# A graph network kernel: two pieces of seven gathers, four slots for edge indices, and node passes in four stages

## The chip, the cores and the metric

The kernel runs on one core of one Trainium2 chip. Its figure is the device time of the whole program in microseconds (us), lower is better. Three runs of the kernel before gave 2862.45 us as median (2857.86 to 2866.96).

## The reference

The graph has 6250 nodes with 128 features and 100000 edges, given as `src` and `dst`, sorted by `dst`, with 16 attributes each. Two layers follow one another, each with a residual and a layer norm around it:

```python
# layer 0: attention over the edges, then a two-layer perceptron per node
q, k, v = X @ Wq, X @ Wk, X @ Wv                      # 8 heads of 16
scores  = einsum(q[dst], k[src]) / sqrt(16)
alpha   = segment softmax of scores over dst
emb     = segment_sum(alpha * v[src], dst) @ W0
h1      = layer_norm(X + emb) * g1 + b1
x       = layernorm(X + layer_norm(h1 + relu(h1 @ fc1 + b) @ fc2 + b) * g2 + b2)
# layer 1: messages; the first 50000 edges use W1f/W2f, the others W1b/W2b
h       = relu(concat(x[src], edge_attr, req) @ W1 + b1) @ W2 + b2
h       = x * (1 + eps) + segment_sum(h, dst) of both halves
out     = layernorm(x + relu(h @ Wu + bu))
```

Both layers read a node's row once per edge (`[src]`) and add into rows by `dst`.

## The kernel before

The edges are cut into chunks of 1792, that is 14 tiles of 128 edges. After a setup (q, k, v of all nodes written to a table in memory, index tables built) three stages follow.

**First loop** (attention, 56 chunks). GpSimd (POOL) issues 14 indirect DMAs per chunk (L657), one per tile of 128 edges, each fetching k and v of 128 source nodes into one of four slots (`RING`). TensorE (PE) expands the queries of a chunk with one matmul per tile (`queries`, L1050), VectorE (DVE) multiplies them with the gathered keys (L1386) and sums by head (L1388), and after some scans by segment weights the values (L1440, two halves). PE then adds the 14 tiles of a chunk into one PSUM area (L1090, a product with a 0/1 mask) and raises `l_agg`; ScalarE (ACT) copies that area (L832). The work of a pass is spread over several chunks: a pass does the scores of `new`, the weights of `b_`, the averages of `c_`. The numbers of `PIECES` (L47) cut a chunk's 14 tiles into four pieces of 4, 3, 4 and 3 tiles. One piece is one pair L1386/L1388, one PSUM bank of queries and one semaphore of the gathers. `gather_chunk` (L643 on) waits ahead of its pieces: for the chunk's indices (`l_ix`) and the second half of the weighted values of the chunk whose slot it takes (`l_pvb`) at the start, for `l_agg` before the second piece, for the queries (`l_q`) before the third, for the turned chunk ends (`l_lr`) before the last.

**Node passes** (10 groups of 5 tiles of nodes). `passes3` runs passes over the groups in three stages on each engine: in one pass `new` gets its embedding matmul (L1132) and first norm, `mid` the perceptron (L1115, ACT relu L868, L1142), `old` the second and third norm, then transposes (L1110), their copy (ACT L903), the product with W1 (L1152), the copy of that (ACT L906) and the store to the table `y_tab` (SP L474). The next pass begins with the transposes of h1 (L1110) and their copy (ACT L881).

**Second loop** (messages, 57 preparations, 56 chunks). POOL gathers rows of `y_tab` (L710), again 14 per chunk into four slots. PE turns the attributes (`attr_T`) and multiplies them with W1 (`attr`, L1187), DVE adds gathered rows and that product (L1575), ACT applies relu (L940), PE adds into rows by `dst` (L1200) and raises `m_agg` behind the last. The indices, columns and attributes of a chunk have two slots. SP loads them: `next_attr` when the attributes of an earlier chunk have been turned, `load_edges(new + 2)` (SP L501, L502) when all four pieces of chunk `new` have been summed (`m_hid`) and its columns read (`m_dcr`). `gather_edges` (L700 on) waits for the indices `m_ix[u]` and for `m_agg` of the chunk that held the slot, before the second piece for `m_eTp` and before the third for `m_u`.

All semaphores, registers and the order on each engine are written out by hand; no planner decides anything.

## Time and profile before

| | |
|---|---|
| median of 3 runs | 2862.45 us |
| profiled execution | 2882.01 us, its span 2880.1 us |
| mean granted TensorE clock | 0.711 of full speed |
| PE matmul / weight load busy | 1588.5 us (55%) / 1255.8 us (44%) |
| DVE / ACT busy | 1430.9 us (50%) / 746.1 us (26%) |
| POOL busy | 1566.9 us (54%) |
| DMA | 255.22 MB, mean 89 GB/s |

The rows below are of the profiled execution. Times there are microseconds from its start. "idle before, releaser" tells how long an engine had been idle ahead of an instruction and what ended it; "issue" is time in which it waited for nothing that the profile shows, "remote" a semaphore whose raiser the profile could not name. An indirect DMA's time on POOL is the time in which it is issued, not that in which the data arrives. One matmul of the program on float32 appears as several instructions.

### The profile page before, as it was taken

The page shows a single profiled execution, that of the slowest core. Times are in us where ns is not written, and L with a number is a line of the kernel's source. Part 1 is how long each engine was busy: PE and PEld are TensorE (multiplying, and loading weights), DVE is VectorE, ACT ScalarE, POOL GpSimd, SP SyncE. Part 2 cuts the span into 40 slices and gives each one's busy share as a digit, 9 for nine tenths or more (in the row PEclk, how much of TensorE's full clock was granted, in tenths as well). Part 3 has the DMA queues.
Part 4 walks back from the last instruction along what each step waited for, and adds up shares of the span by engine and source line. Part 5 has one row for each costly group of instructions (what it writes and reads, how often), then busy time and mean ns, then how long its engine had stood idle before and what let it go on. Part 6 is the DMA issues. An engine that isn't in the chain of part 4 may idle for free.

```text
span 2880.1 us, 32266 instructions
## 1 busy us (share of the span) xinstructions
PE 1588.5 (55%) x7344; PEld 1255.8 (44%) x7345; DVE 1430.9 (50%) x2992; ACT 746.1 (26%) x1502; POOL 1566.9 (54%) x1648
## 2 busy tenths in 40 slices
PE   5315556565556565555777345555555555555546
PEld 3215555555555555554555233333433333333424
DVE  3226666666666666666555234343443333344435
ACT  2213333333333333333454111111111111111111
POOL 3346666666666666663111455655666665556653
PEclk8557676767776777776998667766676666666667
DMA  5474444444444444441000112211221121112211
GB/s 167 138 200 127 143 131 141 131 138 133 129 142 131 141 131 138 133 128 60 18 27 27 56 42 51 52 49 48 54 51 51 50 52 50 47 48 51 53 49 38
DMA packets 148162, 255.22 MB, mean 89 GB/s; under 512 B 73948, under 2 KB 99088, under 8 KB 147996
## 3 DMA queue, kind: packets, MB, share of 16 engines
q0 software_dynamic: 65072, 160.39, 19.9%
...
q8 instruction: 12, 0.20, 0.0%
...
## 4 chain that ended last, share of the span: by engine, by line
issue 33%; PE 22%; DVE 16%; another core or an unknown queue 13%; DVEq 5%; DMA 5%; ACT 4%; SPq 1%; POOL 0%; ACTq 0%; POOLq 0%
PE ps L1090 8%; PE ps L1050 6%; DVE arena L1566 3%; DVE arena L1435 2%; DVE arena L1575 2%; PE ps L1200 2%; DVEq L1595 2%; PE ps L1187 1%; ACT arena L873 1%; PE ps L1152 1%; DVEq L1594 1%; DVE arena L1440 1%; DMA first<-d 1%; DVEq L1592 1%
## 5 line engine op out<-in xcount | busy, mean ns | idle before, releaser
L710 POOL DMA_INDIRECT arena<-y_tab,arena x784 | 741.9, 946 | 512.6 <-issue 494.1
L657 POOL DMA_INDIRECT arena<-kvq_tab,arena x784 | 749.0, 955 | 471.3 <-issue 240.6
L1050 PE MATMUL ps<-arena 128*128 128x128 f32 x1596 | 325.7, 363 | 331.0 <-issue 251.4
L1200 PEld LDWEIGHTS ps<-arena 128*128 128x128 f32 x1568 | 285.5, 247 | 413.2 <-issue 394.1
L1200 PE MATMUL ps<-arena 128*128 128x128 f32 x1568 | 308.0, 336 | 282.8 <-issue 273.5
L1050 PEld LDWEIGHTS ps<-arena 128*128 128x128 f32 x1596 | 299.5, 275 | 349.9 <-issue 345.5
L1090 PE MATMUL ps<-arena 128*128 128x136 f32 x1568 | 319.2, 391 | 173.3 <-DVE arena L1440 88.5
L1090 PEld LDWEIGHTS ps<-arena 128*128 128x128 f32 x1568 | 309.5, 295 | 190.6 <-issue 190.6
L940 ACT ACTIVATE arena<-arena 128x512 f32<-128x512 f32 x224 | 118.9, 567 | 1029.7 <-DVE arena L1575 662.7
L1575 DVE TENSOR_TENSOR arena<-ps,arena 128x512 f32<-128x512 f32 x224 | 127.8, 616 | 511.2 <-remote 299.1
L1187 PE MATMUL ps<-w1blk,eaT 113*128 x456 | 271.3, 677 | 59.4 <-issue 55.6
L809 ACT ACTIVATE arena<-arena 128x1792 f32<-128x1792 f32 x58 | 191.5, 3301 | 0.0
L1568 DVE TENSOR_REDUCE arena<-arena 128x128 f32<-128x1792 f32 x57 | 182.4, 3200 | 2.0
L1404 DVE COPY arena<-arena 8x1 f32<-8x1 f32 x56 | 7.9, 141 | 337.5 <-ACT arena L843 337.5
L832 ACT ACTIVATE arena<-ps 128x136 f32<-128x136 f32 x56 | 16.0, 285 | 507.4 <-remote 476.9
L1388 DVE TENSOR_REDUCE arena<-arena 128x32 f32<-128x512 f32 x224 | 139.2, 621 | 8.4 <-issue 0.5
L1386 DVE TENSOR_TENSOR arena<-ps,arena 128x512 f32<-128x512 f32 x224 | 135.9, 607 | 5.7 <-remote 3.0
L1187 PEld LDWEIGHTS ps<-w1blk,eaT 113*128 113x128 f32 x456 | 90.9, 240 | 75.1 <-issue 74.9
L1566 DVE TENSOR_TENSOR arena<-ps,arena 128x1792 f32<-128x1792 f32 x57 | 114.3, 2006 | 4.8 <-ACT arena L930 4.8
L1440 DVE TENSOR_TENSOR arena<-arena,ps 128x896 f32<-128x896 f32 x112 | 115.6, 1068 | 0.0
L1435 DVE TENSOR_TENSOR arena<-ps,arena 128x1792 f32<-128x1792 f32 x56 | 112.3, 2005 | 0.0
L1601 DVE TENSOR_TENSOR arena<-arena,ps 128x128 f32 x56 | 16.2, 288 | 190.2 <-issue 179.7
...
## 6 DMA issues: line engine op xcount, KB each, us to landing
...
```

The lines of the kernel that those rows point to most:

```text
L657: g.indirect_dma_start(kv_s[:, r, t, :], None, kvq_tab.rearrange("n (a d) -> (n a) d", a=3), bass.IndirectOffsetOnAxis(ap=v3(idx, RING)[:, ...
L710: g.indirect_dma_start(yg_s[:, r, t, :], None, y_tab, bass.IndirectOffsetOnAxis(ap=v3(idx1, 2)[:, u, t:t + 1], axis=0)).then_inc(m_g[r][k] ...
L809: a.activation(hotT.rearrange("n (u g e) -> n u g e", u=2, g=G)[:, u, :, :], line.rearrange("n (e g) -> n g e", g=G), ACT.Relu, scale=-1.0 ...
L1050: last = mm(bank(k)[:, t * D:(t + 1) * D], hotT_s[:, u, s0 + t, :], v3(qwin, 2)[:, u, :])
L1090: last = mm(sums, hot_s[:, u, t, :], contrib_s[:, u, t * RW:(t + 1) * RW], start=(t == 0), stop=(t == G - 1))
L1187: mm(bank(j)[:, 0:n * D], eaT_s[:, u, k * P:(k + 1) * P], w1blk[:, ds(way + a0 * D, n * D)]).then_inc(m_u, 1)
L1200: last = mm(bank(6 + u)[:, 0:W], yg_s[:, r, t, :], hot1_s[:, u, t, :], start=(t == 0), stop=(t == G - 1))
L1435: tt(hot_s[:, u, :, :], columns[:, None, :].to_broadcast([P, G, P]), dcr_s[:, u, :, None].to_broadcast([P, G, P]), ALU.is_equal).then_inc( ...
L1440: tt(contrib_s[:, u, s0:s1, :, 0:DH], kv_s[:, r, s0:s1, D:2 * D].rearrange("p g (h w) -> p g h w", h=H), weights.rearrange("p (g h) -> p g ...
L1566: link(tt(hot1_s[:, u, :, :], columns1[:, None, :].to_broadcast([P, G, W]), dcr1[:, :, None].to_broadcast([P, G, W]), ALU.is_equal))
L1568: v.tensor_reduce(v3(hsum, 2)[:, u, :], hot1_s[:, u, :, :].rearrange("p g n -> p n g"), AX_X, ALU.add).then_inc(m_hot, 1)
L1575: tt(rows_, v3(bank(j)[:, 0:n * D], n), rows_, ALU.add).then_inc(m_hid, 1)
```

## The change

There are three parts.

1. `PIECES` is now two pieces of seven tiles in both loops. A piece's queries or attribute products lie in a pair of PSUM banks, and the DVE and ACT instructions of a piece cover 896 elements per partition in place of 512 or 384. In the first loop PE does the queries of seven tiles ahead of the sums L1090 and seven behind (as before), and DVE's order within a pass changes: `averages`, `steps` and `lanes` now stand ahead of the wait for ACT's exponentials (`l_e`), and one of the two score pieces comes last. `gather_chunk` is not edited, but with two pieces it never comes to its waits ahead of a third and fourth: it waits for `l_ix` and `l_pvb` at the start and for `l_agg` ahead of the eighth tile (the fifth before), and not for `l_q` and `l_lr`.
2. In the second loop the indices, columns and attributes have four slots. SP loads all three of chunk `new + 4` after the hidden rows of chunk `new`, and the first four before the node passes. The gathers of a chunk wait only at its start.
3. The node passes have four stages: the product with W1 of a group (`out_`), its copy and its store are in the pass after that of its last norm. The order within a pass changes on PE, ACT and DVE. POOL's two memsets for the second loop come after its first addition.

The diff, cut to its core. `...` marks what is left out (declarations, the same edits of indices elsewhere, the shape of L1386 and L1575):

```diff
-PIECES = ((0, 4), (4, 3), (7, 4), (11, 3))
+PIECES = ((0, 7), (7, 7))
...
-            with eng.Fori(0, GROUPS - 2) as i:
-                one_pass(i + 2, i + 1, i)
-            one_pass(None, GROUPS - 1, GROUPS - 2)
-            one_pass(None, None, GROUPS - 1)
+            one_pass(0, None, None, None)
+            one_pass(1, 0, None, None)
+            one_pass(2, 1, 0, None)
+            with eng.Fori(0, GROUPS - 3) as i:
+                one_pass(i + 3, i + 2, i + 1, i)
+            one_pass(None, GROUPS - 1, GROUPS - 2, GROUPS - 3)
+            one_pass(None, None, GROUPS - 1, GROUPS - 2)
+            one_pass(None, None, None, GROUPS - 1)
...
+            sp.wait_ge(l_over, 4)
+            sp.wait_ge(s_eac, 32)
+            sp.wait_ge(s_tabi[1], 48)
+            def load_chunk(chunk, r):
+                off = sp.value_load(tab_sb[1][0:1, ds(5 * chunk, 1)], min_val=0, max_val=NB * CH)
+                sp.dma_start(eat_s[:, r, :], ea1[ds(off, CH), :].rearrange("(p g) f -> p (g f)", g=G)).then_inc(m_at[r], 16)
+                sp.dma_start(v3(idx1, RING)[:, r, :], i1[ds(off, CH)].rearrange("(p g) -> p g", g=G)).then_inc(m_ix[r], 16)
+                sp.dma_start(v3(dcol1, RING)[:, r, :], d1[ds(off, CH)].rearrange("(p g) -> p g", g=G)).then_inc(m_ld[r], 16)
+
+            for c in range(RING):
+                load_chunk(c, c)
...
             def sp_msgs(r, new, a_, b_, c_):
                 u = r % 2
                 if new is not None:
-                    next_attr(new + 3, 1 - u)
                     sp.wait_ge(s_eac, 32)
                     sp.wait_ge(m_hid, spent)
-                    sp.wait_ge(m_dcr, prepared)
-                    load_edges(new + 2, u)
+                    load_chunk(new + RING, r)
                     sp.reg_add(spent, spent, NP_)
-                    sp.reg_add(prepared, prepared, 1)
+                    if r == RING - 1:
+                        sp.reg_add(loaded, loaded, 16)
...
             def gather_edges(r):
-                u = r % 2
                 pool.wait_ge(m_buf, 4)
-                pool.wait_ge(m_ix[u], landed)
+                pool.wait_ge(m_ix[r], landed)
                 pool.wait_ge(m_agg, slot_free)
                 for k, (s0, n) in enumerate(PIECES):
-                    if k in (1, 2):
-                        pool.wait_ge(m_buf, 4)
-                        pool.wait_ge(*((m_eTp, turned_) if k == 1 else (m_u, asked)))
                     for t in range(s0, s0 + n):
                         g.indirect_dma_start(yg_s[:, r, t, :], None, y_tab,
-                                             bass.IndirectOffsetOnAxis(ap=v3(idx1, 2)[:, u, t:t + 1], axis=0)).then_inc(m_g[r][k], 16)
+                                             bass.IndirectOffsetOnAxis(ap=v3(idx1, RING)[:, r, t:t + 1], axis=0)).then_inc(m_g[r][k], 16)
                 pool.reg_add(slot_free, slot_free, 1)
-                pool.reg_add(asked, asked, NP_)
...
-            def act_pass(new, mid, old):
+            def act_pass(new, mid, old, out_):
                 if new is not None:
                     a.activation(v3(nTa, GRP), by_tile(new), ACT.Copy).then_inc(n_aT, 1)
                 if mid is not None:
                     act.wait_ge(n_hTp, mid + 1)
                     a.activation(nTh, bank(0, 2)[:, 0:GRP * P], ACT.Copy).then_inc(n_hT, 1)
-                    relu(mid, 0)
                 if old is not None:
                     sqrt(1, old, norm2)
+                if out_ is not None:
+                    act.wait_ge(n_y, out_ + 1)
+                    act.wait_ge(n_yfree, out_ + 1)
+                    y_ = yst[:, ds((out_ % 2) * (GRP * 2 * D), GRP * 2 * D)]
+                    a.activation(y_[:, 0:(GRP - 1) * 2 * D], bank(2, 2)[:, 0:(GRP - 1) * 2 * D], ACT.Copy)
+                    a.activation(y_[:, (GRP - 1) * 2 * D:GRP * 2 * D], bank(1)[:, D:3 * D], ACT.Copy).then_inc(n_ys, 1)
                 if mid is not None:
-                    relu(mid, 1)
-                if mid is not None:
-                    relu(mid, 2)
-                    relu(mid, 3)
+                    for c in range(FC):
+                        relu(mid, c)
                 if old is not None:
                     sqrt(2, old, norm2)
-                if new is not None:
-                    sqrt(0, new, norm1)
-                if old is not None:
                     act.wait_ge(n_r[1], old + 1)
                     normalised(v3(res2, GRP), v3(res2, GRP), norm2).then_inc(n_x1, 1)
                 if new is not None:
+                    sqrt(0, new, norm1)
                     act.wait_ge(n_r[0], new + 1)
                     normalised(v3(res, GRP), v3(res, GRP), norm1).then_inc(n_n1, 1)
                 if old is not None:
                     act.wait_ge(n_xTp, old + 2)
                     act.wait_ge(n_x1c, old + 1)
                     a.activation(nTx, bank(0, 2)[:, 0:GRP * P], ACT.Copy).then_inc(n_xT, 1)
-                    act.wait_ge(n_y, old + 1)
-                    act.wait_ge(n_yfree, old + 1)
-                    a.activation(yst[:, ds((old % 2) * (GRP * 2 * D), GRP * 2 * D)], bank(4, 3)[:, 0:GRP * 2 * D], ACT.Copy).then_inc(n_ys, 1)
...
                 if new is not None:
                     queries(w, 0, True)
-                    queries(w, 1, True)
...
                 if new is not None:
-                    queries(w, 2, True)
-                    queries(w, 3, True)
+                    queries(w, 1, True)
...
-            def pe_pass(new, mid, old):
+            def rows_y(t):
+                return bank(2, 2)[:, t * 2 * D:(t + 1) * 2 * D] if t < GRP - 1 else bank(1)[:, D:3 * D]
+
+            def pe_pass(new, mid, old, out_):
                 if mid is not None:
                     pe.wait_ge(n_h1, mid + 1)
+                    if out_ is not None:
+                        pe.wait_ge(n_xT, out_ + 1)
                     transposes(h1, n_hTp)
+                if old is not None:
+                    pe.wait_ge(n_z, old + 1)
+                if out_ is not None:
+                    pe.wait_ge(n_xT, out_ + 1)
+                    for t in range(GRP):
+                        if t == GRP - 1 and mid is not None:
+                            pe.wait_ge(n_hT, mid + 1)
+                        last = mm(rows_y(t), nTx[:, t * P:(t + 1) * P], w1x[:, :])
+                    last.then_inc(n_y, 1)
+                if mid is not None:
                     pe.wait_ge(n_hT, mid + 1)
-                    pe.wait_ge(n_ys, 1 if old is None else old + 1)
                     hidden(mid, 0)
                     hidden(mid, 1)
-                if mid is not None:
-                    pe.wait_ge(n_f1s, mid * FC + 1)
-                    hidden(mid, 2)
+                if out_ is not None:
+                    pe.wait_ge(n_ys, out_ + 2)
                 if new is not None:
                     pe.wait_ge(n_aT, new + 1)
                     for t in range(GRP):
                         last = mm(bank(0, 2)[0:NT, t * D:(t + 1) * D], nTa[:, t * NT:(t + 1) * NT], w0_sb[:, :])
                     last.then_inc(n_emb, 1)
                 if mid is not None:
-                    pe.wait_ge(n_f1s, mid * FC + 2)
-                    hidden(mid, 3)
-                    pe.wait_ge(n_f1s, mid * FC + FC)
-                    if old is not None:
-                        pe.wait_ge(n_v[1], old + 1)
+                    for c in range(2, FC):
+                        pe.wait_ge(n_f1s, mid * FC + (c - 1))
+                        hidden(mid, c)
                     for t in range(GRP):
+                        if t == GRP - 2 and old is not None:
+                            turn_rows(new, old)
                         for c in range(FC):
+                            if t == 0:
+                                pe.wait_ge(n_f1s, mid * FC + (c + 1))
                             last = mm(bank(2, 2)[:, t * D:(t + 1) * D], v3(ffT, FC)[:, c, t * P:(t + 1) * P], fc2_sb[:, c, :],
                                       start=(c == 0), stop=(c == FC - 1))
                     last.then_inc(n_f2, 1)
-                if old is not None:
-                    if new is not None:
-                        pe.wait_ge(n_v[0], new + 1)
-                    pe.wait_ge(n_x1, old + 1)
-                    transposes(res2, n_xTp)
-                    pe.wait_ge(n_xT, old + 1)
-                    for t in range(GRP):
-                        last = mm(bank(4, 3)[:, t * 2 * D:(t + 1) * 2 * D], nTx[:, t * P:(t + 1) * P], w1x[:, :])
-                    last.then_inc(n_y, 1)
...
```

The change moves instructions in the three places that follow. A row is a line, an operation, the tiles that it writes and reads, and the semaphores it waits for; "x3" means three such in a row.

POOL in the second loop, one chunk's 14 gathers, before and now (`m_ix1` is the semaphore of the index slot, `m_buf` one raised once before the loop):

```order
L710 DMA arena<-y_tab,arena 128x128 [waits m_agg,m_ix1,m_buf]
L710 DMA arena<-y_tab,arena 128x128 x3
L710 DMA arena<-y_tab,arena 128x128 [waits m_eTp,m_buf]
L710 DMA arena<-y_tab,arena 128x128 x2
L710 DMA arena<-y_tab,arena 128x128 [waits m_u,m_buf]
L710 DMA arena<-y_tab,arena 128x128 x6
```
```order
L697 DMA arena<-y_tab,arena 128x128 [waits m_agg,m_ix1,m_buf]
L697 DMA arena<-y_tab,arena 128x128 x13
L699 REGISTER_ALU
L697 DMA arena<-y_tab,arena 128x128 [waits m_agg,m_ix2,m_buf]
L697 DMA arena<-y_tab,arena 128x128 x13
```

The two waits inside the chunk have gone, and each chunk's 14 gathers stand in a row behind one instruction that waits; now two chunks are shown, with other index slots.

DVE in a pass of the first loop, from the wait for `l_e` on before, and from the averages on now (L1412 and L1417 are the averages that were L1426 and L1431, L1353 the steps, L1390 the copy that waits for `l_e`, L1421 the mask, the L1426 of now the weighting that was L1440, L1372 and L1374 the scores that were L1386 and L1388; `...` stands for registers and the rest of the averages and steps):

```order
L1404 COPY arena<-arena 8x1 [waits l_paqc,l_lr,l_e]
...
L1405 SCALAR_TENSOR_TENSOR arena<-arena,ps 8x128 [waits s_dv]
...
L1426 SCALAR_TENSOR_TENSOR arena<-ps,arena 1x136 [waits l_avT,l_ra,l_cur]
...
L1431 TENSOR_TENSOR arena<-arena 128x128 [waits s_dv]
L1367 TENSOR_TENSOR arena<-arena 128x15 [waits l_ld3,s_init]
...
L1435 TENSOR_TENSOR arena<-ps,arena 128x1792 [waits l_dcr]
L1440 TENSOR_TENSOR arena<-arena,ps 128x56x16 x2
L1386 TENSOR_TENSOR arena<-ps,arena 128x4x128 [waits l_q,l_g2_2]
L1388 TENSOR_REDUCE arena<-arena 128x4x8 [waits l_prod]
```
```order
L1412 SCALAR_TENSOR_TENSOR arena<-ps,arena 1x136 [waits l_avT,l_ra,l_cur]
...
L1417 TENSOR_TENSOR arena<-arena 128x128 [waits s_dv]
L1353 TENSOR_TENSOR arena<-arena 128x15 [waits l_ld3,s_init]
...
L1390 COPY arena<-arena 8x1 [waits l_paqc,l_lr,l_e]
...
L1391 SCALAR_TENSOR_TENSOR arena<-arena,ps 8x128 [waits s_dv]
...
L1421 TENSOR_TENSOR arena<-ps,arena 128x1792 [waits l_dcr]
L1426 TENSOR_TENSOR arena<-arena,ps 128x56x16 x2
L1372 TENSOR_TENSOR arena<-ps,arena 128x7x128 [waits l_q,l_g2_1]
L1374 TENSOR_REDUCE arena<-arena 128x7x8 [waits l_prod]
```

The averages and steps now come ahead of the instruction that waits for `l_e`, and behind it the mask and the weighting follow directly on the across-chunk scans.

PE in a steady node pass: before, its end, and now, its beginning (L1142 is the second layer of the perceptron, L1110 and now L1082 are transposes, L1152 and now L1106 the product with W1, L1087 the first layer):

```order
L1142 MATMUL ps<-fc_sb,arena 128x128 [waits n_v1,n_f1s]
L1142 MATMUL ps<-fc_sb,arena 128x128 x19
L1110 MATMUL ps<-ident,arena 128x128 [waits n_x1,n_v0]
L1110 MATMUL ps<-ident,arena 128x128 x4
L1152 MATMUL ps<-w1x,arena 128x256 [waits n_xT]
L1152 MATMUL ps<-w1x,arena 128x256 x4
```
```order
L1082 MATMUL ps<-ident,arena 128x128 [waits n_xT]
L1082 MATMUL ps<-ident,arena 128x128 x4
L1100 REGISTER_ALU
L1106 MATMUL ps<-w1x,arena 128x256 [waits n_xT,n_z]
L1106 MATMUL ps<-w1x,arena 128x256 x3
L1106 MATMUL ps<-w1x,arena 128x256 [waits n_hT]
L1087 MATMUL ps<-arena,fc_sb 128x512 [waits n_hT]
```

The product with W1 has moved from the end of the pass to the place behind the first transposes of the next one, where it serves the group of the pass before. The transposes of the last norm's result (behind L1142 before) now stand inside the second layer's matmuls, ahead of their last eight.

## Rows read from the trace of the kernel before

**Rows 1.** The page: busy time of each engine.
```profile
PE 1588.5 (55%) x7344; PEld 1255.8 (44%) x7345; DVE 1430.9 (50%) x2992; ACT 746.1 (26%) x1502; POOL 1566.9 (54%) x1648
```

**Rows 2.** Busy time by stretch: PE, weight loads, DVE, ACT, POOL; clock, DMA share, GB/s.
```profile
600.00:800.00 200.00, 118.47 (x597) 108.25 (x598) 129.49 (x284) 72.54 (x128) 126.54 (x133) 0.71 0.45 137
1400.00:1600.00 200.00, 137.87 (x703) 103.32 (x703) 104.61 (x396) 95.04 (x172) 25.40 (x18) 0.87 0.08 29
2200.00:2400.00 200.00, 106.54 (x442) 74.67 (x441) 80.72 (x118) 27.64 (x81) 119.85 (x128) 0.67 0.20 50
```

**Rows 3.** Single lines: durations, first and last start, forms.
```profile
L1435 DVE TENSOR_TENSOR arena<-ps,arena x47: 2004/2005/2007, 314.2 to 1280.0; 128x1792 f32<-128x1792 f32 x47
L1566 DVE TENSOR_TENSOR arena<-ps,arena x49: 2004/2005/2006, 1721.8 to 2791.0; 128x1792 f32<-128x1792 f32 x49
L878 ACT ACTIVATE arena<-nodes x7: 1360/1361/1365, 1404.2 to 1543.6; 128x625 f32 x7
```

**Rows 4.** Waits from 300 to 1300 us: total, times, longest.
```profile
ACT arena L832 <- remote: 450.5, 48, 10.3
POOL arena L657 <- remote: 175.5, 48, 3.9
```

**Rows 5.** Timeline of a first-loop cycle: start, duration, instruction, idle before.
```profile
1233.05 0.95 POOL L657 DMA_INDIRECT arena<-kvq_tab,arena  x1 [3.63 <-remote]
...
1235.09 0.14 DVE L1404 COPY arena<-arena 8x1 f32<-8x1 f32 x1 [6.78 <-ACT arena L843]
...
1239.90 2.06 DVE L1440 TENSOR_TENSOR arena<-arena,ps 128x896 f32<-128x896 f32 x2
...
1241.11 5.15 PE L1090 MATMUL ps<-arena 128*128 128x136 f32 x28 [2.84 <-DVE arena L1440]
...
1249.35 0.95 POOL L657 DMA_INDIRECT arena<-kvq_tab,arena  x1 [0.31 <-issue]
1249.43 0.27 PE L1050 MATMUL ps<-arena 128*128 128x128 f32 x1 [1.82 <-issue]
...
1253.28 0.29 ACT L832 ACTIVATE arena<-ps 128x136 f32<-128x136 f32 x1 [9.30 <-remote]
...
1254.04 0.95 POOL L657 DMA_INDIRECT arena<-kvq_tab,arena  x1 [3.74 <-remote]
```

**Rows 6.** Timeline in the second loop, 2162 to 2255 us.
```profile
2162.52 0.37 PE L1200 MATMUL ps<-arena 128*128 128x128 f32 x1 [2.46 <-issue]
...
2186.52 0.34 SPq L501 DMA_DIRECT2D arena<-i  x1
...
2187.22 1.91 PE L1200 MATMUL ps<-arena 128*128 128x128 f32 x8
...
2188.97 0.95 POOL L710 DMA_INDIRECT arena<-y_tab,arena  x1 [8.74 <-issue]
...
2211.45 0.95 POOL L710 DMA_INDIRECT arena<-y_tab,arena  x1 [5.14 <-issue]
...
2254.81 0.95 POOL L710 DMA_INDIRECT arena<-y_tab,arena  x1 [8.65 <-issue]
```

**Rows 7.** Timeline of a steady node pass, 1469 to 1492.5 us.
```profile
1469.65 0.68 ACT L903 ACTIVATE arena<-ps 128x640 f32<-128x640 f32 x1
...
1470.38 2.43 PE L1152 MATMUL ps<-w1x,arena 128*128 128x256 f32 x10 [1.68 <-ACT arena L903]
1470.64 0.83 DVE L1538 TENSOR_TENSOR arena<-arena,rows 128x640 f32<-128x640 f32 x1
...
1472.65 0.71 PE L1110 MATMUL ps<-ident,arena 128*128 128x128 f32 x5
...
1475.38 0.70 ACT L881 ACTIVATE arena<-ps 128x640 f32<-128x640 f32 x1
...
1484.46 4.73 PE L1142 MATMUL ps<-fc_sb,arena 128*128 128x128 f32 x40 [0.89 <-ACT arena L868]
...
1487.87 3.96 ACT L873 ACTIVATE arena<-arena 128x128 f32<-128x128 f32 x10
...
1492.46 1.16 PEld L1152 LDWEIGHTS ps<-w1x,arena 128*128 128x128 f32 x6 [1.92 <-ACT arena L903]
```

**Rows 8.** Timeline where the second loop begins.
```profile
1600.63 0.28 SPq L474 DMA_DIRECT2D y_tab<-arena  x1
1607.44 0.20 ACT L913 ACTIVATE mark<-eps_ln 128x1 f32<-128x1 f32 x1 [7.14 <-DMA y_tab<-arena]
1609.35 0.29 DVE L1562 COPY ps<-iota_row 128x128 f32<-128x128 f32 x1 [10.14 <-issue]
...
1611.82 0.36 SPq L501 DMA_DIRECT2D arena<-i  x1
...
1614.21 0.99 POOL L710 DMA_INDIRECT arena<-y_tab,arena  x1 [18.46 <-DMA arena<-i]
...
1677.69 0.94 POOL L710 DMA_INDIRECT arena<-y_tab,arena  x1 [11.20 <-issue]
```

148 lines of the change are left out of this document (60 added, 88 removed).

## The prediction

> **What bounds the kernel now.** I read the busy times first: no engine is above 55% of the span [rows 1]. By stretch it is the same everywhere: in the first loop POOL is at 126.54 of 200 us and DVE at 129.49, in the second POOL at 119.85 and PE at 106.54, and in the node passes PE at 137.87 [rows 2]. So nothing is full, and what counts is who waits for whom.
>
> First loop. L1435 runs once per chunk: 47 of them from 314.2 to 1280.0 us, so a chunk takes 965.8 / 46 = 21.0 us [rows 3]. POOL waits 48 times, 175.5 us in all, for something "remote", so 3.66 us per chunk, and ACT's copy L832 waits as often and for up to 10.3 us [rows 4]. The timeline shows what that is. POOL resumes at 1233.05 and issues 14 gathers, the last at 1249.35 (14 x 0.95 us with 0.31 between, 17.3 us), then stands until 1254.04 [rows 5]. It waits for `l_agg`: L832, which waits for it too, starts at 1253.28. The matmuls L1090 that raise it are drawn from 1241.11 to 1246.26, 7 us earlier. In between PE's instructions come late, one at 1249.43 after an idle time of 1.82 us, and L832 starts only 3.0 us after the last gather has been issued at 1250.30 [rows 5]. The second loop shows the same more plainly: at 2162.52, inside a run of gathers, a matmul of 0.37 us comes after 2.46 us of nothing, while at 2187.22, with POOL at rest, eight take 1.91 us [rows 6]. So while POOL issues gathers for long, PE crawls, and what waits for PE's semaphores is set free when POOL stops. A chunk costs 14 gathers, 17.3 us, plus the pause that PE needs: 3.7 us in the first loop.
>
> Second loop. L1566 gives (2791.0 - 1721.8) / 48 = 22.3 us per chunk [rows 3]. The pauses are uneven. The starts behind them are 2188.97, 2211.45 and 2254.81: a run of 14 gathers takes 22.48 us with its pause of 5.14, one of 28 takes 43.36 with 8.65, that is 21.68 per 14 [rows 6]. The first run of the loop had 42 and took 1677.69 - 1614.21 = 63.48 us, 21.16 per 14 [rows 6, 8]. What ends the 8.74 us pause is the index load at 2186.52, issued once the hidden rows of the chunk two before were done: POOL starts 2.45 us behind it [rows 6].
>
> Node passes. Seven copies L878 from 1404.2 to 1543.6 give 139.4 / 6 = 23.2 us per pass [rows 3].
>
> **The change part by part.** The profiled execution took 2882.01 us, its span 2880.1; the median of three runs is 2862.45, that is 0.9932 of it. I sum in the profiled time and scale at the end.
>
> *First loop, pieces and waits: 0.* The gathers wait for `l_agg` once per chunk before and now, only ahead of another tile, so a cycle is still 14 gathers and a pause. The waits for `l_q` and `l_lr` that go released nothing late: none of POOL's long waits comes from them [rows 4]. The start of a chunk's gathers, now 7 gathers (8.8 us) after POOL resumes, needs `l_pvb`, the end of L1440. It ended 1241.96 - 1233.05 = 8.9 us after, but DVE now does about 2 us of averages and steps ahead of the wait for `l_e` in which it stood idle for 6.78 us [rows 5], so it ends at about 7. L1090 moves forward by the same 2 us, to end about 11 us after POOL resumes. If its semaphore still comes out only when POOL has stopped, nothing is won. Halving the number of DVE and ACT instructions per piece saves work beside idle time. Bounds: if `l_agg` comes out early, POOL runs on for two or three chunks at a time as in the second loop, at 21.16 to 22.48 per chunk against 21.0 [rows 3, 6, 8], so -0 to +1.4 us by some 52 chunks, at most +77; on the other side a pause shorter by the 2 us of DVE's work would give 52 x 2 = -104. I take 0, because the pause of 48 of 48 cycles is the same.
>
> *Second loop, slots: -39.* POOL no longer waits for an index load behind the hidden rows of the chunk two before. It waits for `m_agg` of the chunk four before, so it may run further ahead. In a pause such as that to 2188.97 the step from SP's load to the first gather (2.45 us) goes, and late in its place is the last L1200 of the older chunk, at about 2187.2 to 2189 [rows 6]. That takes 0 to 2 us from a pause per two chunks, and the share of long runs grows. 42 gathers took 21.16 per 14, 28 took 21.68, 14 took 22.48. I take 21.5 against 22.3 for all but the first and last chunks: 0.75 x 52 = -39. The bounds: 20.5 (17.3 with the 3.2 per chunk left if 2 us go from 5.14) gives 52 x -1.8 = -94; and if every pause were as long as 8.65 behind only 14 gathers (17.3 + 8.65 = 25.95), +190. The price is nearest to the run of 42.
>
> *SP's loads.* Each chunk now loads attributes, indices and columns together after its hidden rows, for a slot that is needed four chunks on. Three issues of 0.34 us stand on SP where POOL no longer listens closely. 0, hidden by the ring. The wait is behind nothing but the output store.
>
> *PE's attributes and the pair of banks.* As many columns and instructions as before. 0.
>
> *Node passes: -33.* The chain of a pass runs from ACT's copy L903 back to itself. Behind L903, which ends at 1470.33, PE does L1152, ACT copies it and the next nodes, and only then comes L881 at 1475.38 [rows 7]: 5.05 us. h1 is there at 1470.64 + 0.83 = 1471.47 and its transposes take 0.71, so L881 could start at 1472.2. With the product in the next pass, behind those transposes, 5.05 becomes about 1.9: -3.2. At the end of the pass ACT did ten L873 of 0.4 us (3.96 us from 1487.87) after all of DVE's statistics; now the five of `old` come first, beside DVE's work on `new`, and -1.4 to -2 is gained, part of which the scale operations between them give back. What is late next is the relus and the second layer, 4.73 us from 1484.46 [rows 7], with the product's 2.43 us now ahead of the first layer, which gives back up to 1 us. I take -4.6 per pass for seven passes, -32, and -1 for the filling, where POOL's first addition no longer stands behind two memsets. The extra pass at the end holds only work that was at the end before: 0. Bounds: -2 per pass (the first layer waits for the product) and -6, so -14 to -43.
>
> *Start of the second loop: -4.* The store of `y_tab` is known to be done at 1607.44, then SP loads attributes, then indices at 1611.82, and the first gather is at 1614.21 [rows 8]. The loads now lie ahead of the node passes, so the gather can follow DVE's L1562 at 1609.35, at about 1609.8: -4.4.
>
> Sum: 2882 + 0 - 39 - 33 - 4 = 2806, times 0.9932 = 2787; I forecast 2785 us.
>
> The Trainium skill ("SBUF — State Buffer", section "SBUF: two separate sides") says that engine ports and DMA ports are disjoint, and that neither a DMA nor a compute operation can slow the other. This trace does not bear it out for PE beside POOL's gathers: a matmul of 0.37 us comes after an idle 2.46 us in a run of gathers, and eight in 1.91 us outside one [rows 6]. By the rule a PE wait would not depend on POOL; the rival D below is what that gives.
>
> **The rivals.**
>
> A. The loops do not gain. The pauses are PE's drain, not the index load, and each is as long as before. For it: the pause grows with the length of the run (5.14 behind 14, 8.65 behind 28 [rows 6]), so running ahead costs what it brings. Against it: the 2.45 us between SP's load and POOL. Then only node passes and start count: 2862 - 37 = 2825.
>
> B. Slower: POOL is no longer held back, and PE crawls longer. Place: both loops. In the first the earlier L1090 gets its semaphore out before PE slows down, POOL runs on for 28 gathers, and a chunk costs 22.0 in place of 21.0: +1.0 x 52 = +52. In the second POOL is always a full ring ahead, so it is set free one chunk at a time and pays a pause behind each 14, the 5.14 of the row and some 0.5 because the last piece is now seven tiles (23.0 in place of 22.3): +0.7 x 52 = +36. Less 37: 2862 + 88 - 37 = 2913. It decides from about +0.7 us per chunk in both loops on. For it: runs of 14 are the dearest per gather in the second loop and L1090 now ends about 2 us earlier. Against it: none of the 48 pauses of the first loop was missed [rows 4].
>
> C. Running ahead pays more: 20.8 us per chunk in the second loop gives 52 x -1.5 = -78, and half a microsecond less pause in the first gives -26; with the node passes 2862 - 104 - 37 = 2721, taken as 2735.
>
> D. PE and DMA do not disturb each other, POOL's 14 gathers of 1.25 us are the only floor: 17.5 per chunk in both loops, 52 x (3.5 + 4.8) = -432, so about 2400. The crawl in rows 5 and 6 speaks against it.
>
> E. The four stages do not shorten a pass, because ACT's order is as tight as before, and the loops stay: 2858.
>
> **How the numbers follow.** Forecast 2785 (2755 to 2812): 0.40. A: 0.21. B: 0.20. C: 0.13. D: 0.02. E: 0.04. A measurement of this kernel can tell 0.3% (9 us) from no change. Faster by more is the forecast, A but for a small tail, C, D and a part of B that ends below 2854: 0.75. Slower by more is most of B: 0.19. Within it: E and the tails, 0.06. The range of 2710 to 2900 holds forecast, A, E, most of C and the lower half of B.
>
> **What would show it.** First loop: L1435's successor still every 21.0 us, with 14 gathers per run and a pause near 3.7; runs of 28 would show B. Second loop: no gather behind an index load, fewer runs of 14, under 21.8 us per chunk. Node passes: seven to eight passes at 18 to 19.5 us, with the relus or the second layer in the waits. First gather of the second loop 2 to 3 us after the store is known to be done. I am wrong if the interval in either loop moves by more than 1 us, since that weighs more than the node passes.

## The result and the profile after

The changed kernel takes 2906.88 us (median of four runs, 2884.57 to 2919.74), the kernel before 2860.84 (2857.86 to 2866.96): ratio 1.015, 95% interval 1.008 to 1.022. It is slower, where I had forecast 2785 us. The execution whose trace is read here took 2899.43 us with a span of 2897.2.

Three stretches tell where it went. The rows are POOL's gathers of the first loop, ACT's node copies and POOL's gathers of the second loop in the profile after (count, shortest, median and longest in ns, then first and last start). L649, L858 and L697 are what L657, L878 and L710 were.

```profile
L649 POOL DMA_INDIRECT arena<-kvq_tab,arena x784: 942/948/1157, 113.7 to 1431.3; - x196
L858 ACT ACTIVATE arena<-nodes x10: 1358/1362/1372, 1479.4 to 1626.3; 128x625 f32 x7, 128x625 f32<-128x625 f32 x3
L697 POOL DMA_INDIRECT arena<-y_tab,arena x784: 941/947/1072, 1687.6 to 2848.2; - x196
```

From the first gather to the first node copy it is 1365.6 us (1242.5 before, from 112.9 to 1355.4), from there to the second loop's first gather 208.2 (258.8), from there to the end 1209.6 (1265.9). So the first loop lost 123, the node passes won 51, the second loop 56: with 1 us at the start that is the 17 us between the two spans. The runs' medians differ by 46. The profiled execution of before was a long one: its 2882.01 us lie 15 above the longest of the four timed runs (2866.96), while the profiled one of the changed kernel is the second fastest of its four. So these stretches understate the loss and overstate one gain. Later runs tell how much: kernels below that keep the second loop of before took 1254.5, 1255.2 and 1251.6 us for it (e11, e14, e17), and those with four pieces and the old waits took 1225.8 to 1229.9 for the first loop (e12, e15, e16). Against these the first loop lost 136 to 140 us, the second won 42 to 46, and the node passes 52 to 53, which gives about 41 of the 46.

**First loop.** The waits between 300 and 1400 us (total, times, longest) show two new ones and one in place of the 175.5 us of [rows 4]:

```profile
ACT ps L821 <- remote: 290.8, 24, 15.5
...
POOL arena L649 <- DVE arena L1426: 174.3, 36, 9.2
...
POOL arena L649 <- remote: 46.9, 16, 3.4
```

The even pause of 3.7 us for `l_agg` [rows 4] has become uneven and rarer: ahead of a chunk's eighth tile POOL stops 23 times, for 2.4 to 6.2 us (the last row has 16 of them, the profile puts the others down to PE). At the start of a chunk it waits for DVE's weighting L1426 (`l_pvb`), 36 times and up to 9.2 us. The timeline of one such cycle (start, duration, instruction, idle before):

```profile
526.70 0.95 POOL L649 DMA_INDIRECT arena<-kvq_tab,arena  x1 [9.10 <-DVE arena L1426]
...
529.94 0.29 ACT L812 ACTIVATE arena<-ps 128x136 f32<-128x136 f32 x1 [2.87 <-PE ps L1063]
...
531.41 0.27 PE L1039 MATMUL ps<-ident,arena 128*8 128x128 f32 x1
...
546.49 0.36 ACT L821 ACTIVATE ps<-arena 128x112 f32<-128x112 f32 x1 [15.53 <-remote]
...
547.29 0.14 DVE L1390 COPY arena<-arena 8x1 f32<-8x1 f32 x1 [10.47 <-ACT arena L823]
...
548.17 1.99 DVE L1421 TENSOR_TENSOR arena<-ps,arena 128x1792 f32<-128x1792 f32 x1
...
550.09 2.06 DVE L1426 TENSOR_TENSOR arena<-arena,ps 128x896 f32<-128x896 f32 x2
...
552.97 0.95 POOL L649 DMA_INDIRECT arena<-kvq_tab,arena  x1 [9.03 <-DVE arena L1426]
```

Here the `l_agg` copy (L812) comes promptly, 3.2 us after POOL resumed. What is held is the next semaphore, `l_lr`: PE's transposes that raise it (L1039) are drawn at 531.41, and ACT's exponentials, which wait for it and for nothing else that is late, start at 546.49. POOL's last gather was over at 543.94 (552.97 - 9.03), 2.6 us earlier. Only then come exponentials, scans, mask and weighting, 6.5 us in all, and POOL, which has gathered its 14 tiles without a stop, needs just these weighted values to begin the next chunk. A cycle is 26.3 us: 17.2 of gathers and 9.05 of pause. Between such cycles lie stretches of the old kind, as this one:

```profile
674.11 0.95 POOL L649 DMA_INDIRECT arena<-kvq_tab,arena  x1 [2.56 <-remote]
...
681.73 0.95 POOL L649 DMA_INDIRECT arena<-kvq_tab,arena  x1 [0.30 <-DVE arena L1426]
...
694.77 0.95 POOL L649 DMA_INDIRECT arena<-kvq_tab,arena  x1 [2.88 <-remote]
```

They take 20.7 us, a little less than before; the weighted values come in just as the seventh gather begins (681.62 and 681.73), one before they are needed. But in the first loop's chunks 12 to 55, 30 of 44 times the weighted values came after POOL could have begun with them (slack: end of the gather before, plus the 0.3 us between two, less the end of L1426's second half), 15 times more than 5 us after. In the trace of before the slack was 3.2 to 4.7 us and never negative. The first 56 gathers also ran in one piece, followed by a pause of 56 us, where before there were 21, 28 and 7: the 57th comes 126.1 us after the first (105.8 before). What cut the first 56 before was the wait for the queries (`l_q`), ahead of a third piece. In the trace of before:

```profile
143.40 0.95 POOL L657 DMA_INDIRECT arena<-kvq_tab,arena  x1 [4.18 <-remote]
...
206.32 1.09 POOL L657 DMA_INDIRECT arena<-kvq_tab,arena  x1 [28.13 <-PE ps L1050]
```

**Node passes.** Two copies that open steady passes, 17.19 us apart (23.2 before [rows 3]):

```profile
1574.70 1.36 ACT L858 ACTIVATE arena<-nodes 128x625 f32 x1
...
1576.74 2.43 PE L1106 MATMUL ps<-w1x,arena 128*128 128x256 f32 x10
1576.87 0.71 ACT L861 ACTIVATE arena<-ps 128x640 f32<-128x640 f32 x1 [0.80 <-PE ps L1082]
...
1586.07 2.05 ACT L853 ACTIVATE arena<-arena 128x128 f32<-128x128 f32 x5 [0.45 <-DVE arena L1483]
...
1591.31 0.68 ACT L884 ACTIVATE arena<-ps 128x640 f32<-128x640 f32 x1
...
1591.89 1.36 ACT L858 ACTIVATE arena<-nodes 128x625 f32 x1
```

**Second loop.** The first gather follows the known end of the table's store by 2.0 us (6.8 before [rows 8]), and the pauses have shrunk from 5.1 and 8.7 us [rows 6] to these:

```profile
1678.80 0.28 SPq L489 DMA_DIRECT2D y_tab<-arena  x1
1685.62 0.20 ACT L891 ACTIVATE mark<-eps_ln 128x1 f32<-128x1 f32 x1 [7.15 <-DMA y_tab<-arena]
...
1687.62 0.99 POOL L697 DMA_INDIRECT arena<-y_tab,arena  x1 [13.76 <-PEq L299]
...
2161.95 0.94 POOL L697 DMA_INDIRECT arena<-y_tab,arena  x1 [6.89 <-PE ps L1188]
...
2204.80 0.94 POOL L697 DMA_INDIRECT arena<-y_tab,arena  x1 [3.42 <-remote]
```

Per 14 gathers the loop takes (2848.2 - 1687.6) / 783 x 14 = 20.75 us, against 22.08 before.

### The profile page after: what moved, and what is told of

Its sections match the earlier page's. It is cut to its first block, busy times and chain, and to the rows that moved or that the text cites. A ratio compares the mean times of both kernels' runs of the same rounds, so it can differ in the third digit from the quotient of the medians.

```text
span 2897.2 us, 30489 instructions
## 1 busy us (share of the span) xinstructions
PE 1518.2 (52%) x7344; PEld 1194.1 (41%) x7345; DVE 1404.2 (48%) x2656; ACT 731.3 (25%) x1399; POOL 1565.3 (54%) x1647
## 4 chain that ended last, share of the span: by engine, by line
another core or an unknown queue 32%; issue 22%; DVE 21%; PE 9%; DMA 5%; ACT 4%; DVEq 4%; SPq 2%; ACTq 1%; POOL 1%; PEldq 0%; POOLq 0%
DVE arena L1547 3%; DVE arena L1421 3%; DVE arena L1426 2%; DVE arena L1372 2%; PE ps L1188 2%; DMA arena<-d 2%; DVE arena L1556 1%; PE ps L1087 1%; PE ps L1063 1%; DVE arena L1374 1%; ACT arena L784 1%; DVEq L1575 1%; DMA first<-d 1%; DVEq L1574 1%
## 5 line engine op out<-in xcount | busy, mean ns | idle before, releaser
L649 POOL DMA_INDIRECT arena<-kvq_tab,arena x784 | 747.4, 953 | 598.1 <-issue 268.8
L697 POOL DMA_INDIRECT arena<-y_tab,arena x784 | 742.4, 947 | 432.9 <-issue 232.5
L1188 PE MATMUL ps<-arena 128*128 128x128 f32 x1568 | 321.0, 358 | 354.7 <-issue 313.5
L1188 PEld LDWEIGHTS ps<-arena 128*128 128x128 f32 x1568 | 287.1, 264 | 418.0 <-issue 351.1
L1063 PEld LDWEIGHTS ps<-arena 128*128 128x128 f32 x1568 | 306.8, 288 | 192.6 <-issue 192.5
L1024 PE MATMUL ps<-arena 128*128 128x128 f32 x1596 | 246.2, 309 | 141.1 <-issue 87.8
L919 ACT ACTIVATE arena<-arena 128x896 f32<-128x896 f32 x112 | 106.1, 947 | 771.4 <-DVE arena L1556 463.2
L1024 PEld LDWEIGHTS ps<-arena 128*128 128x128 f32 x1596 | 229.7, 223 | 152.2 <-issue 150.6
L1556 DVE TENSOR_TENSOR arena<-ps,arena 128x896 f32<-128x896 f32 x112 | 119.3, 1087 | 308.0 <-remote 193.1
L1047 PE MATMUL ps<-ident,arena 8*128 8x8 f32 x56 | 12.8, 229 | 416.8 <-DVE arena L1392 327.4
L1047 PEld LDWEIGHTS ps<-ident,arena 8*128 8x128 f32 x56 | 9.2, 165 | 427.2 <-issue 427.2
L1372 DVE TENSOR_TENSOR arena<-ps,arena 128x896 f32<-128x896 f32 x112 | 120.2, 1073 | 127.5 <-remote 125.6
L1569 DVE BATCH_NORM_STATS2 arena<-ps 128x6 f32<-128x128 f32 x56 | 16.4, 292 | 241.7 <-remote 238.0
L1374 DVE TENSOR_REDUCE arena<-arena 128x56 f32<-128x896 f32 x112 | 121.9, 1088 | 3.8
L812 ACT ACTIVATE arena<-ps 128x136 f32<-128x136 f32 x56 | 16.0, 286 | 412.8 <-PE ps L1063 211.5
L1426 DVE TENSOR_TENSOR arena<-arena,ps 128x896 f32<-128x896 f32 x112 | 115.5, 1067 | 0.0
L1547 DVE TENSOR_TENSOR arena<-ps,arena 128x1792 f32<-128x1792 f32 x57 | 114.3, 2005 | 0.2 <-ACT arena L909 0.2
```

The source lines that it names most:

```text
L649: g.indirect_dma_start(kv_s[:, r, t, :], None, kvq_tab.rearrange("n (a d) -> (n a) d", a=3), bass.IndirectOffsetOnAxis(ap=v3(idx, RING)[:, ...
L697: g.indirect_dma_start(yg_s[:, r, t, :], None, y_tab, bass.IndirectOffsetOnAxis(ap=v3(idx1, RING)[:, r, t:t + 1], axis=0)).then_inc(m_g[r] ...
L1024: last = mm(bank(2 * k, 2)[:, t * D:(t + 1) * D], hotT_s[:, u, s0 + t, :], v3(qwin, 2)[:, u, :])
L1063: last = mm(sums, hot_s[:, u, t, :], contrib_s[:, u, t * RW:(t + 1) * RW], start=(t == 0), stop=(t == G - 1))
L1188: last = mm(bank(6 + u)[:, 0:W], yg_s[:, r, t, :], hot1_s[:, u, t, :], start=(t == 0), stop=(t == G - 1))
L1372: tt(keys, v3(bank(2 * k, 2)[:, 0:n * D], n), keys, ALU.mult).then_inc(l_prod, 1)
```

## The experiments

At first there are two theories of the first loop's loss. W: the waits for `l_q` and `l_lr` that the gathers lost had kept POOL in step, though they released nothing late. O: the new order on DVE causes it. Three more come later. P: the wait for `l_agg` moved from a chunk's fifth to its eighth tile. Z: the pieces of seven themselves. B (not the rival B of the prediction): it takes both edits of the waits together. Times are of the profiled executions where a stretch is named, of all runs where a ratio is. The kernels ran in seven groups (the first is the result above), each group on one chip and the six of the experiments on six different ones, so ratios are to the kernel before on the same chip. The outcome ahead of the detail: the loss of the first loop needs both edits of the waits, and a chip on which PE's semaphores are held back; neither the pieces of seven nor DVE's order is to blame.

**On two chips nothing is held back.** The next group had four kernels: e1, the changed kernel with the whole first loop of before (`PIECES0` of four for the first loop, `PIECES1` of two for the second, DVE and PE in the old order); e2, one wait more in `gather_chunk`:

```diff
 for t in range(s0, s0 + n):
+    if t == 11:
+        pool.wait_ge(s_init, 3)
+        pool.wait_ge(l_lr, turned_)
```

e3, `averages`, `steps` and `lanes` back behind `dve.wait_ge(l_e, minus2)` and `across`; e4, the kernel before with

```diff
-                    if k == 2:
-                        pool.wait_ge(l_q, asked)
-                    if k == 3:
-                        pool.wait_ge(l_lr, turned_)
```

Expected of e1: 

> The changed kernel with its first loop as it was before (four pieces of 4, 3, 4, 3 tiles, the order of before on DVE and PE, so also the gathers' waits for l_q and l_lr); second loop and node passes as changed. The changed kernel's stages were, against before: first loop +124 us, node passes and start of the second loop -51, second loop -56. Every theory of the first loop: 21.0 us per chunk, node passes begin near 1355 us, no POOL pause of 9 us, total 2860 - 51 - 56 = about 2755 (2740 to 2775). If the stages were not independent, for instance if the second loop gained only because of how the first left the engines, it would be 2790 or more.

Of e2: 

> The changed kernel with one wait more: ahead of a chunk's twelfth gather POOL waits for l_lr again, as before the change. Theory W (the lost pacing wait): POOL stops behind 11 gathers, PE's semaphore comes out, the 9.05 us pauses behind the weighted values go, first loop at 20.8 to 21.5 us per chunk, total 2760 to 2800. Theory O (the new order on DVE and the pieces of seven put the semaphores at the wrong time): still many cycles of 26.3 us, total 2880 to 2910.

Of e3: 

> The changed kernel with DVE's order in the first loop as before (averages, steps and lanes behind the wait for l_e); pieces of seven and no pacing waits. Theory O: the 26.3 us cycles go, total 2760 to 2800. Theory W: they stay, first loop 22 to 23 us per chunk or more, total 2890 to 2930 (some 2 us more in each of the long cycles, since the averages again stand in the chain that POOL waits for).

Of e4: 

> The kernel before without the two waits of the first loop's gathers for l_q and l_lr, nothing else. Theory W: cycles with POOL pauses of about 9 to 11 us behind the weighted values appear, first loop 22 to 24 us per chunk, total 2920 to 3000. Theory O: within 0.5% of 2860, since those waits released nothing late in the trace of before.

Measured: the kernel before itself took 2434.09 us there; e1 0.978 of it (0.976 to 0.981), e2 0.980 (0.978 to 0.981), e3 0.980 (0.978 to 0.982), e4 0.999 (0.998 to 1.000). None of the times expected came out, since behind its first 56 gathers POOL never paused. The changed kernel, e5, was then run on another chip. 

> The changed kernel itself, beside the kernel before, on the chip of this call. In the four runs so far on another chip (first loop restored, a wait restored, DVE order restored, and the kernel before without its pacing waits) POOL never paused in either loop and the kernel before took 2434 us in place of 2861. Theory S (the change's first loop loses only where PE's semaphores are held back during the gathers, which that chip doesn't do): on a chip with 17.5 us per chunk the changed kernel takes 2380 to 2386 us, 50 us less than before; on one with 21.0 us per chunk for the kernel before, about 2900, 40 us more. Theory I (the first loop's change is itself slower): over 2434 us even without the hold.

It took 2383.47 us, 0.979 (0.976 to 0.981), as theory S had it. In its trace the first loop's gathers and POOL's waits from 300 to 1100 us are

```profile
L649 POOL DMA_INDIRECT arena<-kvq_tab,arena x784: 944/947/1160, 116.1 to 1132.0; - x196
```

```profile
POOL arena L649 <- DVE arena L1426: 8.8, 29, 0.3
```

The loop runs at 17.6 us per chunk behind its first 56 gathers, with nothing between gathers but the usual 0.3. Against e4 (the kernel before but for two waits) the stretches are 1054.6 to 1051.5, 206.3 to 259.0 and 1003.9 to 1003.5 us: without the hold the change to the loops is worth nothing, and the node passes give it all. All later groups ran on chips where the kernel before takes 2859 to 2888 us, and where the hold is seen.

**Node passes alone (e6)**: the kernel before with the new `passes3`, `act_pass`, `pe_pass`, `dve_pass` and `pool_pass`. 

> The kernel before with the four-stage node passes alone. In the two profiled pairs (one on each chip) the stretch from the first node copy to the first gather of the second loop shortened from 258.8 to 208.2 us and from 259.0 to 206.3. A part of that is the index and attribute loads that now lie ahead, which this kernel does not have. Theory N (passes of 23 us become passes of 18 to 18.5): 40 to 48 us less than the kernel before, and the first gather of the second loop 4 to 5 us later behind the table's store than in the changed kernel. Rival (the gain is the earlier loads and memsets): under 15 us less.

2835.04 us, 0.981 (0.978 to 0.984), 53 us less than before, on a chip where the kernel before takes 2888.19. The stretch of the node passes is 211.1 us; the second loop keeps its 1265.5. Theory N: the stretch is 47.7 us shorter, and the interval (45 to 64 us of the whole time) reaches into its 40 to 48.

**A made-up hold (e7, e8).** PE waits, ahead of the transposes behind `l_lr`, for a semaphore that POOL raises behind a tile (13 in e7, 10 in e8, where POOL's wait of e2 is in too):

```diff
                     pe.wait_ge(l_ml, minus1)
+                    if new is not None:
+                        pe.wait_ge(s_init, 3)
+                        pe.wait_ge(p_run, held)
```

> The changed kernel with a made-up hold in the first loop: PE may do the transposes behind l_lr of a chunk only when POOL has issued all 14 gathers of the chunk two later. This copies, on a chip that does not hold PE's semaphores back, what the trace of the changed kernel shows in its 26.3 us cycles. Theory W: POOL's pause is then the whole chain behind l_lr (exponentials 0.8, scans 1.0, mask 2.0, weighting 2.1, some 6.4 us in all with the waits): 23.5 to 24.5 us per chunk, total 2383 + 52 x 6.5 = about 2720 (2670 to 2760). Theory O: the chain is covered by POOL's lead and the first loop stays under 19 us per chunk.

> The same with the wait of before given back: POOL stops ahead of its twelfth gather for l_lr, and PE's hold ends when 11 gathers have been issued. Theory W: three gathers (3.75 us) now lie beside the chain behind l_lr, 20 to 21.3 us per chunk, some 3 to 4 us less than with the hold over 14, total about 2540 (2510 to 2590). Theory O: no difference between the two.

They fell on a chip that holds by itself, so the absolute times expected do not apply: 2900.18 and 2843.51 us in one run each, 1.004 and 0.985 of before. First loop 1365.0 and 1312.5 us. e7 is like the changed kernel without the hold added (1365.6), so making the hold certain adds nothing to what the chip does. That doesn't tell W from the others by itself. e8 beside e7 is the first sign that a stop behind 11 gathers helps, in one run each.

**The same edits where the hold acts (e9 to e12)** are e2, e3, e4 and e1. 

> Again the changed kernel with POOL's wait for l_lr ahead of the twelfth gather, for a chip that holds PE's semaphores back (kernel before near 2860 to 2890 us). Theory W: no pauses of 9 us behind the weighted values, first loop at 20.8 to 21.5 us per chunk, 3 to 4% under the kernel before. Theory O: 1 to 2% over the kernel before, as the changed kernel. On a chip without the hold: 2.1% under before, which tells nothing.

> Again the changed kernel with DVE's order of before in the first loop. Theory W: the long pauses stay and grow by the 2 us of averages and steps (11 us behind 14 gathers, 28 us per such cycle), 2 to 5% over the kernel before. Theory O: they go, 3 to 4% under it. Without the hold: 2.1% under.

> Again the kernel before without its waits for l_q and l_lr. Theory W: pauses of 9 to 11 us behind the weighted values in part or all of the first loop, 2 to 8% over the kernel before. Theory O: within 0.5%. Without the hold: within 0.2%.

> Again the changed kernel with the first loop of before. With the hold: first loop 21.0 us per chunk, node passes and second loop as changed (-51, -56), 3.5 to 4% under the kernel before. Without it: 2.2% under.

Measured: e9 2822.84 us, 0.988 (0.985 to 0.991), first loop 1289.5 us. e10 2929.95 (2875.70, 2922.58, 2937.32 and 2945.94, too far apart for an interval): the median is 1.025 of before, the fastest run 1.006; first loop 1387.9 in the run of 2922.58. e11 2891.45, 1.011 (1.007 to 1.016), first loop 1248.0. e12 2761.13, 0.965 (0.963 to 0.967), first loop 1228.8. O falls: with the old order the changed kernel is no better, not even in its fastest run, where O has 3 to 4% under before. e12 comes out at 3.5%, the least that the stretches promised. W is right only in half, and its 3 to 4% for e9 and 2 to 8% for e11 were both missed (so was O's 0.5% for e11): `l_lr` given back wins 79 us of the 140 between the changed kernel (at the ratio 1.015) and e12, and taken from the kernel before it costs 33, but not through pauses of 9 us. In e11 every pause behind the first 56 gathers is 3.3 to 4.8 us, and only the start is longer: 56 gathers in one piece and 122.5 us to the 57th (105.0 in e12). In e9 the long pause is cut in two. POOL's waits from 300 to 1300 us:

```profile
POOL arena L652 <- remote: 84.4, 33, 3.4
POOL arena L652 <- DVE arena L1429: 57.1, 31, 2.5
POOL arena L652 <- PE ps L1066: 52.5, 17, 6.3
```

In such a cycle it stops behind 11 gathers for 2.9 us (19 times behind the start of the loop), which lets `l_lr` out, issues three more beside the chain, and stops 2.3 us for the weighted values: 22.1 us per chunk in place of 26.3.

**Where the wait for `l_agg` stands (e13, e14), and the pieces (e15).** e13 is the changed kernel with

```diff
-                    if k == 1:
-                        pool.wait_ge(l_agg, slot_free)
                     for t in range(s0, s0 + n):
+                        if t == 4:
+                            pool.wait_ge(s_init, 3)
+                            pool.wait_ge(l_agg, slot_free)
```

e14 the kernel before with `l_agg` awaited at `k == 2` in place of `k == 1`; e15 is e12 with DVE's new order. 

> The changed kernel with POOL's wait for l_agg ahead of a chunk's fifth tile, as before, in place of the eighth; all else as changed. Theory P (place of the wait): POOL resumes on l_agg with ten gathers left in the chunk, so the weighted values are needed 12.5 us later and not 8.75 us; they come after 7 to 9 us, so they are never late, the 26.3 us cycles go, first loop at 20.7 to 21 us per chunk; 2.6 to 3.4% under the kernel before (the first 56 gathers may stay 10 to 17 us longer). Theory Z (pieces of seven): 1 to 2% over the kernel before. On a chip without the hold both give 2.1% under.

> The kernel before with the wait for l_agg moved from the fifth to the eighth tile; its waits for l_q and l_lr stay, four pieces stay. Theory P: the weighted values (ready 8.9 us behind the resumption in the trace of before) come later than the 8.75 us at which they are then needed, POOL stops at chunk starts, cycles of 11 + 3 gathers as in the run with the l_lr wait given back: 21.5 to 22.5 us per chunk, 1 to 3% over the kernel before. Theory Z: within 0.5%. Without the hold: within 0.2%.

> The changed kernel with the first loop in four pieces (with all its waits at their old tiles) but DVE's new order (averages, steps and lanes ahead of the wait for l_e). Theory P: no 26.3 us cycles; POOL's pause is set by when PE's semaphore comes out, so 20.7 us per chunk, within 0.3% of the kernel with the whole first loop of before, that is 3.5% under the kernel before. If the order matters: more than 1% away from that.

Measured: e13 2797.56, 0.976 (0.974 to 0.979), just short of P's 2.6 to 3.4%; e14 2877.18, 1.005 (1.003 to 1.008); e15 2762.63, 0.965 (0.963 to 0.967). In e13 one wait's place takes the 9 us pauses away but for three of 7 to 9.3 us near the start; POOL's long waits are again all for `l_agg`:

```profile
POOL arena L650 <- remote: 151.3, 44, 3.6
```

Its first loop is 1266.3 us, 37 over e12, of which 22 lie ahead of the 57th gather (126.6 to 105.0). In e14 no 9 us pause appears: in chunks 12 to 55 the slack of the weighted values is 0.1 to 1.9 us in place of 3.2 to 4.7, and never negative in the profiled execution. So P alone doesn't make the cycle either, and its 1 to 3% for e14 was missed. e15 says that DVE's new order is harmless, and worth nothing.

**Both waits at once (e17, e18).** e17 is the kernel before, four pieces, with both edits of the waits:

```diff
-                    if k == 1:
-                        pool.wait_ge(l_agg, slot_free)
                     if k == 2:
-                        pool.wait_ge(l_q, asked)
-                    if k == 3:
-                        pool.wait_ge(l_lr, turned_)
+                        pool.wait_ge(l_agg, slot_free)
```

e18 is the changed kernel, two pieces, with all three waits at their old tiles:

```diff
                     for t in range(s0, s0 + n):
+                        if t in (4, 7, 11):
+                            pool.wait_ge(s_init, 3)
+                            pool.wait_ge(*{4: (l_agg, slot_free), 7: (l_q, asked), 11: (l_lr, turned_)}[t])
```

> The kernel before with four pieces, whose gathers wait as in the changed kernel: for l_agg ahead of the eighth tile, and not for l_q and l_lr. Theory B (both edits of the waits together make the 26 us cycles): POOL pauses of 9 us or more behind the weighted values in a good part of the first loop, 22 to 24 us per chunk, 2 to 6% over the kernel before. Theory Z (the pieces of seven are needed): no such pauses behind the first 56 gathers, at most 1.2% over it, as with one edit at a time.

> The changed kernel with pieces of seven and the gathers' three waits at the tiles where they were (l_agg ahead of the fifth, l_q of the eighth, l_lr of the twelfth). Theory B: first loop as in the kernel with the whole first loop of before, 20.7 us per chunk, and with the waits back the first 56 gathers are interrupted again: within 0.4% of 2762 us, that is 3.5% under the kernel before. Theory Z: more than 1% over that, with 9 us pauses.

e17: 3013.05, 3025.41, 3145.34 and 3148.77 us, again without an interval; the two faster runs are 1.054 and 1.058 of before, the median of all four 1.079. The profiled one is the fastest. Why two took 130 us more no run tells, so 5% is what may be put down to the edits. e18: 2757.16 us, 0.964 (0.962 to 0.965). Theory B. POOL's waits from 300 to 1400 us in e17, and from 300 to 1290 in e18:

```profile
POOL arena L653 <- DVE arena L1436: 173.2, 28, 11.0
POOL arena L653 <- remote: 75.7, 25, 3.4
```

```profile
POOL arena L646 <- remote: 164.3, 48, 3.6
```

With both edits and nothing else the kernel before pauses up to 11.0 us for the weighted values, and loses more, even in its fastest run, than either edit costs (1.1% and 0.5%) or both together; with both undone and nothing else the changed kernel is as fast as e12 and e15. The long cycles are not there from the start of e17's steady part: in chunks 12 to 35 it runs like e14, at 20.8 us per chunk with a slack of 0.0 to 2.0 us, then the slack of chunk 36 is -5.7 us and long cycles follow to the end of the loop, with short breaks at chunks 45 and 54. A slack so thin holds for a while, and what tipped it here the trace does not show.

**The second loop (e16)**: e12 and one wait more at the start of a chunk's gathers, `pool.wait_ge(m_hid, asked)`, for the hidden rows of the chunk two before. 

> The kernel with the first loop of before and all else as changed, and in the second loop one wait more: the gathers of a chunk wait for the hidden rows of the chunk two before (m_hid), as the index load had to. It ties POOL's lead as before but without the load's latency. Theory L (latency of load and issue, 2.45 us behind each such wait, is what went): 21.0 to 21.4 us per chunk in the second loop, 20 to 35 us over the kernel without this wait. Theory R (lead: POOL may be a chunk further ahead): 22 us per chunk as before the change, 55 us over it. If the wait is never the last: equal, 20.7 us per chunk.

2815.08 us, 0.983 (0.982 to 0.985); by the ratios 53 us over e12. The second loop is 1254.3 us (1208.5 in e12, 1265.9 before). Theory R, whose figure was 55 us. Between 1700 and 2700 us:

```profile
POOL arena L702 <- DVE arena L1570: 203.7, 29, 13.9
```

e14 ran beside it on the same chip with the second loop of before and took 1255.2 us for it. So the wait for hidden rows alone takes back the whole gain of that loop, 46 us against e12: the gain is POOL's lead, and for the load behind that wait, now issued earlier, nothing is left.

## Why the prediction was wrong

*What bounds the kernel* held in five of the seven groups, the result's among them: a chunk costs 14 gathers and pauses, and what is late behind PE is set free when POOL stops. The first loop was lost by this very mechanism. In the other two there is no pause behind the first 56 gathers.

*First loop, pieces and waits: 0* is the step that failed. It measured +123 us against the profiled execution of before, 136 to 140 against the later runs. I had two facts in hand and put them together wrongly. I saw that `l_pvb` is needed 8.8 us after POOL resumes, in place of 12.5, and reckoned it to be ready after 7: a slack of 1.8 us where 3.6 had been. In the short cycle at 674.11 it was ready after 7.5 (L1426 ended at 681.62), 1.4 us before it was needed, in the next cycle 0.5 us before, in the one behind that 0.5 us after, and there the long cycles begin. Once it is late, POOL begins a chunk on `l_pvb` and not on `l_agg`, and from there runs 14 gathers without having to stop for PE, since `l_agg` has come by the eighth tile. Then the next thing held is `l_lr`, at the head of the chain to the next `l_pvb`. This order of events is read from the trace; that it takes both edits of the waits is what e11, e14, e17 and e18 show. I asked whether `l_agg` would still come out late, not what else hangs on a PE semaphore once it does not. And I wrote that the waits for `l_q` and `l_lr` released nothing late. That was read from 300 us on [rows 4]. At the start of the loop `l_q` did stop POOL, for 4.2 and 28.1 us, and without these stops the 57th gather comes some 20 us later (126.1 us in the changed kernel, 122.5 in e11 and 126.0 in e17, which have no wait for `l_q`, against 105.8 before and 101.8 in e14, which has it). From 300 us on it is true, but with the wait for `l_agg` late the other two matter: e14 has them and is 0.5% slower than before, e17 lacks them and is at least 5%. How they help was seen only in e9, where the one for `l_lr` stops POOL inside the chunk; in e14's profiled execution POOL never stops for 1 us or more at that wait, and `l_q` and `l_lr` were not tried apart there.

*The rivals.* Rival B came nearest in time (2913 against 2907) and named both loops, the first rightly, but by a wrong way, so the nearness is luck: it had runs of 28 at 22.0 us per chunk, where the trace has runs of 14 at 26.3 in part of the loop, and a slower second loop where it got faster. D, POOL's gathers as the only floor, is what two chips do, though there the kernel before needs only 2436 us too, so the change wins 2.1% and not D's 430 us. The Trainium skill ("SBUF — State Buffer", section "SBUF: two separate sides") says that a DMA and a compute operation cannot slow each other; the traces of those two chips agree, with 17.5 to 17.6 us per chunk, those of the other groups do not, by the rows at the end.

*Second loop: -39.* It measured -56 against the profiled execution of before, -42 to -46 against the later runs: 20.75 us per chunk in place of the 21.5 taken. The mechanism named first, the index load's 2.45 us, earned nothing that can be seen; e16 gives the gain to POOL's lead.

*Node passes: -33.* A pass takes 17.2 us, 6.0 less, where I took 4.6, so the saving of a pass was mis-sized. The stretch to the second loop's first gather shortened by 50.6, of which the loads ahead of the passes are 4.8 (6.8 to 2.0 us behind the store, forecast 4.4) and the rest, 46, the passes; e6 confirms that (-47.7 for the stretch). The product is no longer in the way: L1106 runs at 1576.74 beside L861. The normalisation of `old` now runs beside DVE's work on `new` as taken. PE's granted clock was 0.95 of full speed in the stretch below (columns as in [rows 2]), 0.87 before [rows 2], so it stood at the higher of its two levels (2.4 GHz) more of the time. Over the whole of the node passes it was 0.90 (1479.4 to 1687.6 us) and 0.84 before (1355.4 to 1614.2). How much of the gain that is, no run separated.

```profile
1500.00:1680.00 180.00, 138.85 (x824) 109.05 (x822) 120.01 (x453) 111.35 (x209) 35.00 (x21) 0.95 0.09 33
```

*SP's loads, PE's attributes*: 0 each. For PE's attributes no run is against it. For SP's loads there is one sign: I had written that no gather of the second loop would wait behind an index load, and between 1700 and 2800 us four do, for 4.0 to 5.0 us each:

```profile
POOL arena L697 <- DMA arena<-i: 18.1, 4, 5.0
```

Whether POOL would have stood as long for something else no run tells. The scaling by 0.9932 was not to be had for the changed kernel: its profiled execution was the second fastest of four, not one above all of them.

The sum of the other steps was -76. It measured -107 against the profiled execution of before, and -98 by e12, which leaves the first loop alone. With the first loop of before the kernel takes 0.965 (e12), with the three waits at their old tiles 0.964 (e18): that is the version to keep.
